# Graph attention layers with windows of 128 edges in place of 256, destination terms spread by a bf16 one-hot in three pieces, and another order of VectorE's work

## The reference

```python
def _gat_layer(x, src, dst, W, a_src, a_dst, b, heads, concat):
    h = (x @ W).reshape(n, heads, -1)
    al_s = jnp.einsum('nhf,hf->nh', h, a_src)
    al_d = jnp.einsum('nhf,hf->nh', h, a_dst)
    e = jax.nn.leaky_relu(al_s[src] + al_d[dst], NEG_SLOPE)
    m = jax.lax.stop_gradient(jax.ops.segment_max(e, dst, num_segments=n))
    ex = jnp.exp(e - m[dst])
    denom = jax.ops.segment_sum(ex, dst, num_segments=n)
    alpha = ex / (denom[dst] + 1e-16)
    out = jax.ops.segment_sum(h[src] * alpha[:, :, None], dst, num_segments=n)
```

## Time and profile before

| what | value |
|---|---|
| median of 3 runs | 5946.67 us (5943.93 to 5946.69) |
| the profiled execution's own time | 5953.62 us |
| its span in the trace | 5952.0 us |
| edge phase of layer 1, first gather to last addition | 324.5 to 2505.7 us |
| edge phase of layer 2, first gather to last addition | 2760.4 to 4959.5 us |
| busy time GpSimd / TensorE / VectorE / ScalarE | 3721 / 4059 / 3247 / 451 us |
| mean granted TensorE clock | 0.745 |

### The profile page before, as it was taken

How to read it: one execution, slowest core, us unless ns; L and a number is a source line. 1 busy time by engine, 2 the same in 40 slices (tenths; PEclk the granted TensorE clock), 3 DMA queues, 4 the chain that set the end, 5 groups by cost and what they waited for, 6 DMA issues and landing times. The chain is left out here.

```text
span 5952.0 us, 71925 instructions
## 1 busy us (share of the span) xinstructions
PE 4058.6 (68%) x16160; PEld 3204.0 (54%) x16161; DVE 3247.2 (55%) x6273; ACT 450.7 (8%) x1938; POOL 3721.4 (63%) x4222
## 2 busy tenths in 40 slices
PE   3557777777777777653777777777777773209990
PEld 2346566666666566532666666666666663206770
DVE  3356666666666666533666656656665664503444
ACT  1100000000000000031000000000000001202220
POOL 1167777777777777512777777777777772161116
PEclk9987777777777777755777777777777775559995
DMA  2144444444444444304444444444444444121216
GB/s 69 52 108 127 127 128 128 126 127 129 126 127 128 128 127 127 97 31 148 128 126 127 126 126 126 128 126 126 126 127 126 126 127 141 50 86 60 64 61 174
DMA packets 311066, 679.50 MB, mean 114 GB/s; under 512 B 76141, under 2 KB 134047, under 8 KB 310746
## 3 DMA queue, kind: packets, MB, share of 16 engines
q0 software_dynamic: 182736, 501.44, 30.5%
q1 hardware_dynamic: 114590, 159.76, 10.3%
q10 hardware_dynamic: 13708, 17.94, 0.9%
HBM read 611.99 MB, written 68.45 MB: 114 GB/s over the span
## 5 line engine op out<-in xcount | busy, mean ns | idle before, releaser
L857 POOL DMA_INDIRECT rows<-table,idx x3328 | 3290.3, 989 | 950.5 <-issue 887.3
L915 PE MATMUL bank<-rows,hit 128*128 128x260 f32 (+1 forms) x6656 | 2434.7, 544 | 625.8 <-DVE acc L976 625.7
L915 PEld LDWEIGHTS bank<-rows,hit 128*128 128x128 f32 x6656 | 1844.4, 284 | 1084.8 <-DVE acc L976 632.4
L903 PE MATMUL bank<-du,hit_t 128*128 x6656 | 866.3, 263 | 535.0 <-DVE hit_t L946 519.7
L903 PEld LDWEIGHTS bank<-du,hit_t 128*128 128x128 f32 x6656 | 832.8, 203 | 698.6 <-issue 698.2
L965 DVE TENSOR_TENSOR rows<-rows,bank 128x2048 f32<-128x2048 f32 x416 | 947.4, 2277 | 1.6 <-ACT rows L875 1.6
L976 DVE TENSOR_TENSOR acc<-acc,bank 128x260 f32 (+1 forms) x1664 | 703.9, 423 | 289.9 <-DVE acc L976 275.3
L957 DVE TENSOR_TENSOR arg<-rows,bank 128x32 f32<-128x32 f32 (+1 forms) x416 | 73.8, 177 | 1369.8 <-DMA rows<-table,idx 1364.3
L935 DVE TENSOR_TENSOR hit<-bank,dst_loc 128x1024 f32<-128x1024 f32 x416 | 506.0, 1217 | 0.1
L874 ACT ACTIVATE bank<-arg 128x32 f32<-128x32 f32 (+1 forms) x416 | 79.3, 191 | 4183.4 <-DVE arg L960 4183.4
L946 DVE TENSOR_SCALAR hit_t<-loc,node_in_tile 128x1024 f32<-128x1024 bf16 x416 | 313.8, 755 | 47.5 <-DMA loc<-loc_row 45.7
(11 more groups left out here) (184 smaller groups left out, 2039.8 us busy)
## 6 DMA issues: line engine op xcount, KB each, us to landing
loc<-loc_row SPq DMA_DIRECT2D x416, 256.0 KB, 3.6
rows<-table,idx POOLq DMA_INDIRECT x3328, 2.8
sent<-zeros SPq DMA_DIRECT2D x1, 13568.0 KB, 48.3
xe<-sent SPq DMA_DIRECT2D x106, 128.0 KB, 2.1
back<-ye POOLq DMA_DIRECT2D x106, 128.0 KB, 2.0
fw<-in_L_ffn_W ACTq DMA_DIRECT2D x16, 512.0 KB, 10.4
table<-acc POOLq DMA_DIRECT2D x49, 130.0 KB, 2.4
table<-acc POOLq DMA_DIRECT2D x49, 128.5 KB, 2.5
```

The lines of the kernel that those rows point to most:

```text
L857: pool.indirect_dma_start(rows[:, way, n, 0:R], None, table, bass.IndirectOffsetOnAxis(idx[:, way, n:n + 1], 0)).then_inc(rows_in[way], 16)
L903: last = nc.tensor.matmul(du_bank[:, n * 2 * H:(n + 1) * 2 * H], hit_t[:, way % 2, n, :], eb.du[:, t, 0:2 * H], start=True, stop=True)
L915: last = nc.tensor.matmul(sum_bank[m][:, 0:R], hit[:, way, n, :], rows[:, way, n, 0:R], start=(g == 0), stop=(g == G - 1))
```

## The change

- Windows have 128 edges (`W`, so `G` = 1): an item is one chunk, a step still has 8 chunks, and there are 202 steps per layer. The plan then has 13 blocks in place of 7, and every one of the eight chunks of a step has its own addition to `acc`.
- `shift_phase` splits the destination terms into three bf16 pieces (`du3`). The transposed one-hot is bf16, each chunk's spreading matmul has 24 columns in layer 1 (6 in layer 2), two PSUM banks take turns, and `keep_du` on VectorE adds the three pieces up.
- The transposed one-hot moves from VectorE to ScalarE, as two activations: |loc - node|, then relu(1 - that).
- The last of the four small operations of `make_arg` (the minimum with 0) moves to ScalarE as well, as a relu.
- `make_hit` is cut into four pieces and `scale_rows` into two; the weights have one buffer in place of two; `make_hit` runs two steps ahead, no longer three.
- The `Carrier` ahead of the gathers is gone: the wait stands on a register.
- VectorE's additions of the step before stand between the small operations and the pieces of `make_hit`. TensorE sums the first four chunks, spreads the terms of step s+2, and sums the last four.

```diff
-W = 256
+W = 128
 G = W // P
 WINDOWS = -(-E // W)
 WROWS = -(-WINDOWS // 16) * 16
-STEP_ITEMS = 4
-ST = STEP_ITEMS * G
-STEPS = -(-(WINDOWS + NT - 1) // (2 * STEP_ITEMS)) * 2
-ITEMS = STEPS * STEP_ITEMS
+ST = 8
+SPLIT = 14
+STEPS = -(-(WINDOWS + NT - 1) // (2 * ST)) * 2
+ITEMS = STEPS * ST
...
+                left = eb.du[:, 0:NT, 0:2 * H]
+                for piece in range(3):
+                    part = eb.du3[:, 0:NT, piece, 0:2 * H]
+                    done.then_wait(nc.vector.tensor_copy(part, left))
+                    if piece < 2:
+                        done.then_wait(nc.vector.tensor_tensor(left, left, part, ALU.subtract))
...
-        weight = [kp.bank[way][:, 0:ST * H].rearrange("p (n h) -> p n h", n=ST) for way in range(2)]
-        du_bank = kp.bank[2]
-        col = kp.bank[3][:, 0:P]
+        weight = kp.bank[0][:, 0:ST * H].rearrange("p (n h) -> p n h", n=ST)
+        col = kp.bank[1][:, 0:P]
+        du_edge = kp.bank[1][:, P:P + ST * 2 * H].rearrange("p (n c) -> p n c", n=ST)
+        du_bank = kp.bank[2:4]
+        du_kept = b.sem(f"du_kept_{layer}")
...
-                met = Carrier(pool, nc.gpsimd, kp.cell[:, 2:4], b.sem(f"gather_waits_met_{layer}"))
+                freed = pool.alloc_register(f"pool_rows_freed_{layer}")
+                pool.reg_mov(freed, ST)
 
                 def gather(s, way, turn):
+                    if not number(s):
+                        rows_freed = pool.snap(freed, min_val=ST, max_val=ITEMS)
                     pool.wait_ge(idx_ready, s + 1)
-                    if not number(s) or s >= SETS:
-                        pool.wait_ge(summed, (s - SETS + 1) * STEP_ITEMS)
-                    met.after_waits(s)
+                    if not number(s):
+                        pool.wait_ge(summed, rows_freed)
+                        pool.reg_add(freed, freed, ST)
+                    elif s >= SETS:
+                        pool.wait_ge(summed, (s - SETS + 1) * ST)
                     for n in range(ST):
...
+                def make_hit_t(s, way, pair):
+
+                    act.wait_ge(loc_in[way % 2], (pair + 1) * 16)
+                    if not number(s) or s >= 1:
+                        act.wait_ge(hit_t_ready, s)
+                    nc.scalar.activation(gap[:, :], loc[:, way % 2, :], ACT.Abs, bias=kp.minus_node[:, 0:1]
+                                         ).then_inc(gap_ready, 1)
+                    act.wait_ge(gap_ready, s + 1)
+                    if not early(s):
+                        act.wait_ge(spread, s - 1)
+                    nc.scalar.activation(hit_t[:, way % 2, :, :].rearrange("p n e -> p (n e)"), gap[:, :], ACT.Relu,
+                                         bias=kp.ones[:, 0:1], scale=-1.0).then_inc(hit_t_ready, 1)
...
-                    nc.scalar.activation(weight[way % 2], arg[:, way % 2, :, :], ACT.Exp).then_inc(weight_ready, 1)
-                    nc.scalar.activation(rows[:, way, :, D:D + H], arg[:, way % 2, :, :], ACT.Exp
-                                         ).then_inc(weight_ready, 1)
+                    nc.scalar.activation(a, a, ACT.Relu, scale=-1.0).then_inc(bounded, 1)
+                    act.wait_ge(bounded, s + 1)
+                    nc.scalar.activation(weight, a, ACT.Exp, scale=-1.0).then_inc(weight_ready, 1)
+                    nc.scalar.activation(rows[:, way, :, D:D + H], a, ACT.Exp, scale=-1.0).then_inc(weight_ready, 1)
...
-                    if not number(s) or s >= 1:
-                        pe.wait_ge(arg_ready, s)
-                    for m in range(STEP_ITEMS):
-                        t = pe.snap(t_regs[m], min_val=0, max_val=NT)
-                        for g in range(G):
-                            n = m * G + g
-                            last = nc.tensor.matmul(du_bank[:, n * 2 * H:(n + 1) * 2 * H],
-                                                    hit_t[:, way % 2, n, :], eb.du[:, t, 0:2 * H],
-                                                    start=True, stop=True)
+                    if not early(s):
+                        pe.wait_ge(du_kept, s - 1)
+                    for n in range(ST):
+                        t = pe.snap(t_regs[n], min_val=0, max_val=NT)
+                        last = nc.tensor.matmul(du_bank[way % 2][:, n * 6 * H:(n + 1) * 6 * H],
+                                                hit_t[:, way % 2, n, :], eb.du3[:, t, :, 0:2 * H],
+                                                start=True, stop=True)
                     last.then_inc(spread, 1)
...
+                def sum_rows(s, way, chunks):
+                    for n in chunks:
+                        if n % PIECE == 0:
+                            pe.wait_ge(scaled, s * PIECES + n // PIECE + 1)
+                        if not number(s) or s * ST + n >= 4:
+                            pe.wait_ge(added, s * ST + n - 3)
+                        nc.tensor.matmul(sum_bank[n % 4][:, 0:R], hit[:, way, n, :], rows[:, way, n, 0:R],
+                                         start=True, stop=True).then_inc(summed, 1)
 
                 def step(s, way, turn):
-                    if not number(s) or s + 1 < STEPS:
-                        spread_du(s + 1, (way + 1) % SETS)
-                    sum_rows(s, way)
+                    sum_rows(s, way, range(0, 4))
+                    if not number(s) or s + 2 < STEPS:
+                        spread_du(s + 2, (way + 2) % SETS)
+                    sum_rows(s, way, range(4, ST))
...
-                def make_hit_t(s, way, pair):
-
-                    dve.wait_ge(loc_in[way % 2], (pair + 1) * 16)
-                    if not early(s):
-                        dve.wait_ge(spread, s - 1)
-                    nc.vector.tensor_single_scalar(hit_t[:, way % 2, :, :].rearrange("p n e -> p (n e)"),
-                                                   loc[:, way % 2, :], kp.node[:, 0:1], ALU.is_equal
-                                                   ).then_inc(hit_t_ready, 1)
...
+                def keep_du(s, way):
+                    dve.wait_ge(spread, s + 1)
+                    if not number(s) or s >= 1:
+                        dve.wait_ge(arg_ready, s)
+                    spread_out = du_bank[way % 2][:, 0:ST * 6 * H].rearrange("p (n k c) -> p n c k", n=ST, k=3)
+                    nc.vector.tensor_reduce(du_edge, spread_out, AX.X, ALU.add).then_inc(du_kept, 1)
...
-                    done.then_wait(nc.vector.tensor_tensor(a, rows[:, way, :, D:D + H], du[:, :, 0:H], ALU.add))
-                    done.then_wait(nc.vector.scalar_tensor_tensor(a, a, SLOPE, a, ALU.mult, ALU.max))
-                    done.then_wait(nc.vector.tensor_tensor(a, a, du[:, :, H:2 * H], ALU.subtract))
-                    nc.vector.tensor_single_scalar(a, a, 0.0, ALU.min).then_inc(arg_ready, 1)
-
...
+                    follows = not number(s) or s >= 1
+                    ahead = not number(s) or s + 1 < STEPS
+                    far = not number(s) or s + 2 < STEPS
+                    nxt, later = (way + 1) % SETS, (way + 2) % SETS
+                    if follows:
+                        dve.load(t_regs, eb.tile_of[0:1, bass.ds((s - 1) * ST, ST)])
+                        add_sum(s - 1, 0)
+                    if far:
+                        make_hit(s + 2, later, 0)
+                    if follows:
+                        add_sum(s - 1, 1)
+                    if far:
+                        make_hit(s + 2, later, 1)
+                    if follows:
+                        add_sum(s - 1, 2)
+                    if ahead:
+                        keep_du(s + 1, nxt)
+                    if follows:
+                        add_sum(s - 1, 3)
+                    for stage in range(3):
+                        if ahead:
+                            make_arg(s + 1, nxt, turn + (way + 1) // SETS, stage)
+                        if follows:
+                            add_sum(s - 1, 4 + stage)
+                    if far:
+                        make_hit(s + 2, later, 2)
+                    if follows:
+                        add_sum(s - 1, 7)
+                    if far:
+                        make_hit(s + 2, later, 3)
+                    if ahead:
+                        for piece in range(PIECES):
+                            scale_rows(s + 1, nxt, piece)
```

146 lines of the change are left out of this document (74 added, 72 removed).

## The result

| | before | after |
|---|---|---|
| median | 5946.68 us (5943.93 to 5946.90, 4 runs) | 5678.85 us (5678.62 to 5679.14, 4 runs) |
| profiled execution, own time / span | 5953.62 / 5952.0 us | 5679.14 / 5677.2 us |
| mean granted TensorE clock | 0.745 | 0.749 |

The ratio is 0.9551, with a 95% interval of 0.9534 to 0.9567: faster by 268 us on the medians, 275 on the two spans. The forecast was 5701, so the gain came out 22 us larger, inside the range. Profiled execution against profiled execution the sum of -246 was 29 us short: 7 of them drop out of the comparison of medians, since the profiled execution of before was 7 us slower than its median and that of the changed kernel was not.

What follows compares the result with a forecast made beforehand. GpSimd's eight gathers, end to end, were taken to set each edge step's pace. Gathers -286 and small costs +40 gave -246 us; 5707.6 from the profiled execution, 5701 us against the median, range 5672 to 5770.

Steps and rivals of the forecast that it cites:

- steps: fewer, long gather, the Carrier's gap: GpSimd's gathers in both edge phases: 202 steps for 208 (-125), no long gather (-133), no border addition (-28), together -286 us.
- plan: Before the edge phases: 13 writes each of `tile_row` and `loc_row` in place of seven, +26 us (15 to 35).
- split in three: In `shift_phase`: five operations, each waited for, to split the destination terms, 4.5 us, put at +4.
- ends of the edge phases: After the last rows land: more additions and sums in alternation, about +4 us a layer, +8 (0 to 14).
- late start of layer 2: Head of layer 2, where `loc` lands after 44 us: two activations in place of a comparison, +2 us.
- The long gather: One gather per step runs 0.33 us longer beside VectorE's comparison with a constant; removing it saves 404 x 0.33 = 133 us.
- The Carrier: GpSimd's addition at each step's border; without it the gap shrinks by 0.07 us, 404 times, -28 us (at worst +40).
- VectorE: Its work per step grows from 6.7 to 8.4 us, still under the 10.01 us step, leaving 1.6 us.
- (1): Rival: the long gather stays, from another cause or other operations; -133 falls away, 5834 us, chance 0.06.
- (2): Rival: VectorE and TensorE get out of step, a step takes 10.3 us, +120, 5821 us, chance 0.06.
- (4): Rival: the register wait makes the step's border cost 0.3 us more than the Carrier, +149, 5850 us, chance 0.04.
- Rival 3: VectorE becomes the bound of the edge phases, 10.94 us a step, +376, 6077 us, chance 0.04.

Runs made afterwards that it cites:

- an edit outside the change: Changed kernel with layer 2's one 13.6 MB clearing DMA replaced by 64 KB with each step and the rest after the last: 5656.68 us, ratio 0.9507.

## Why the prediction was right, and where its terms were off

On the spans, in the order of the prediction's sum:

| term | forecast | measured | from |
|---|---|---|---|
| steps: fewer, long gather, the Carrier's gap | -286 | -292 | step 10.003 us for 10.415; both gather stretches, without layer 2's stop |
| the Carrier outside the steps | none | -16 | -7, -12, +3 at its three places |
| plan | +26 | +16 | timeline below |
| split in three | +4 | +4 | +2.6 and +1.3 |
| ends of the edge phases | +8 | +7 | last gather's end to last addition 14.8, after 18.2 |
| late start of layer 2 | +2 | +7 | stop of 18.6 us, after 24.2, and slower restart |
| sum | -246 | -274 | span -275 |

- *What bounds the kernel* was read rightly, and by the view that decides it: gathers end to end with only "issue" ahead of them. (The waits in the earlier trace rows are those of 400 to 2480 us, 199 steps, so VectorE waited 3.2 us a step, not 3.3.) It explains at once why the bf16 pieces and the new order of VectorE measured as nothing.
- *The long gather*, -133 in 404 steps: the one-hot on ScalarE alone gave -130 in 416, where 0.33 us makes -137. Taking 0.33 from whole steps and not the overlap of 0.47 was right; by the rule of the Trainium skill on SBUF — State Buffer, in "Who interferes with whom", that the other engine is blocked until the comparison is done, it would have been -190. The trace agrees with the rule only from 0.13 us after the gather's start, and not for a comparison that begins in the last 0.10 us ahead of a gather.
- *The Carrier* is the term that failed. The prediction priced it at 0.07 us a border, -28 us, and looked for it nowhere else. With it back in the changed kernel the time rose by 41 to 45 us: 33 in the steps (the gather behind it is longer too) and 17 outside them, less the 6 by which layer 2's stop got shorter. The row was in the trace of before: the Carrier of layer 1 with 26.97 us of idling put down to "issue", 7.4 us after its indices.
- *The plan* was sized from the seven writes of each kind, taken as serial. The writes of `tile_row` overlap, as the earlier trace rows could have told, with seven issued in 3.19 us and the last landed by 35.25: 13 of them are through 15.5 us after the first was issued (23.15 to 38.70), where seven took 14.1. The 13 of `loc_row` cost the 2 us each that were laid out. This is the case that the prediction had named as its low end, 15. The plan's queue after, which answers to the earlier trace rows:

```profile
23.15 6.04 SPq L286 DMA_DIRECT2D tile_row<-tile_i  x13
...
38.70 0.24 SPq L289 DMA_DIRECT2D tile_of<-tile_row  x1
...
40.52 25.83 SPq L296 DMA_DIRECT2D loc_row<-loc  x13
```

- *The late start of layer 2* was priced as if `loc` came a fixed time after the gathers begin. It comes a fixed time after the clearing begins, and the clearing did not start later; so an earlier first gather gains nothing, and 7 us are lost. The whole stop of 24 us was there to be had with an edit outside the change.
- *VectorE*: 8.4 of 10.0 us and a wait of 1.5 to 2 us a step were forecast; the wait is 2.4. The durations do sum to 8.4 us a step, and the reduction takes the 0.36 us laid out for it; but in the trace an operation's record often begins before the one ahead of it has ended, so VectorE is busy for 1373.93 / 190 = 7.2 us a step in 400 to 2300. That sum was too high by this overlap of 1.1 us. The activations take 1.15 us (forecast 1.1) and the gaps ahead of the additions come to 0.35 us a step.
- *The rivals.* The long gather does not stay (1), the engines do not get out of step (2), the border is no longer than the rest (4). Rival 3 exists, but only with some 2.6 us more of work.
- *The range* held by 7 us, and partly by luck. Its low end had room for a cheaper plan (11 us, and 10 came), for cheaper ends (8, and 1 came) and for the rounding of the step (10). What used up the rest was the 21 us that the Carrier gave beyond its term, for which no room had been made, less the 5 of the stop in layer 2; and 7 us of the profiled execution of before do not show in the medians.

## What to carry to other kernels

When one engine stands end to end, price an edit by what it does to that engine's own rows, and by what on another engine holds it up; reordering and cheaper data types on the others bought slack here and no time. Give idle time that is put down to "issue" a second look at the first instruction of a phase, not only in the loop: a one-column addition on GpSimd cost as much there as in 200 steps. And where a phase starts with a large transfer in the queue of the small ones that it needs, spread the large one over the steps.
